# Moving one block's attention and its addition behind the first two tiles of the gated layer

## What is computed

```python
Q, K, V = x @ wq.T, x @ wk.T, x @ wv.T              # width 64
context = (Q @ (K.T V as D x D "energy")) * sqrt(3 / 64)
x = layernorm(x + context @ wo.T)
h = silu((x @ w1.T) * w1_s) * ((x @ w2.T) * w2_s)   # width 1024
h = gelu((h @ h1.T) * h1_s)                         # exact gelu
h = gelu((h @ h2.T) * h2_s)
x = layernorm(x + (h @ w3.T) * w3_s)
```

## Time and profile before

| | us |
|---|---|
| median of 3 runs | 651.08 |
| lowest and highest run | 650.98 to 651.11 |
| profiled run, whole | 650.84 |
| profiled run, span of the core | 649.0 |
| TensorE, products: busy | 637.2 (98%) |
| TensorE, weight loads: busy | 535.3 (82%) |
| VectorE busy | 492.3 (76%) |
| ScalarE busy | 408.6 (63%) |
| GpSimd busy | 282.5 (44%) |

### The profile page before, as it was taken

The page is one execution under the profiler, slowest core; times in us unless marked ns, Lnnn a source line. Parts: engine busy times, 40 slices in busy tenths (PEclk is TensorE's granted clock), DMA queues, the critical chain, the costliest instruction groups (busy, mean ns, idle before and its releaser), DMA issues.

```text
span 649.0 us, 9260 instructions
## 1 busy us (share of the span) xinstructions
PE 637.2 (98%) x3191; PEld 535.3 (82%) x3191; DVE 492.3 (76%) x721; ACT 408.6 (63%) x692; POOL 282.5 (44%) x226
## 2 busy tenths in 40 slices
PE   8989999999999999999999999999999999999995
PEld 6868788878879888888889888888879888888885
DVE  4677989989564997789655898698754899488476
ACT  5479689768671566558662657656763457566654
POOL 0367999493000762096000565078000367069025
PEclk9999999999999999999999999999999999999999
DMA  8998998973310046534330035634330015534201
GB/s 328 397 374 311 359 369 313 358 264 131 132 67 1 2 157 214 179 131 138 130 123 1 0 98 181 256 123 154 131 130 1 1 25 186 179 130 156 105 1 68
DMA packets 24371, 103.91 MB, mean 160 GB/s; under 512 B 2224, under 2 KB 3312, under 8 KB 16496
## 3 DMA queue, kind: packets, MB, share of 16 engines
q1 hardware_dynamic: 24032, 102.98, 44.7%
q10 hardware_dynamic: 288, 0.26, 0.1%
HBM read 87.51 MB, written 23.07 MB: 170 GB/s over the span
## 4 chain that ended last, share of the span: by engine, by line
PE 88%; DVE 5%; issue 2%; ACT 2%; DMA 1%; POOL 1%; SPq 0%; POOLq 0%; ACTq 0%; DVEq 0%
PE ps L1338 56%; PE ps L1281 17%; PE ps L1407 8%; DVE R L950 3%; PE ps L1181 2%; PE ps L1213 1%; PE ps L1164 1%; DMA xT<-in_xT 1%; PE ps L1430 1%; PE ps L1201 1%; ACT R L682 1%; PE ps L1189 1%; ACT junk L575 1%; POOL rstd L494 0%; DVE st L921 0%
## 5 line engine op out<-in xcount | busy, mean ns | idle before, releaser
L1338 PE MATMUL ps<-R,ring 128*128 128x512 f32 x1792 | 410.2, 390 | 0.2 <-DVE fsum L870 0.2
L1338 PEld LDWEIGHTS ps<-R,ring 128*128 128x128 f32 x1792 | 335.2, 188 | 69.9 <-DVE fsum L870 0.6
L950 DVE TENSOR_TENSOR R<-quarter,R 128x512 fp32r<-128x512 f32 x284 | 262.7, 948 | 57.3 <-ACT R L682 56.9
L682 ACT CAST R<-quarter 128x512 fp32r<-128x512 f32 x284 | 173.2, 617 | 30.3 <-POOL quarter L522 12.3
L1281 PE MATMUL ps<-x1T,w 128*128 128x512 f32 x512 | 119.1, 391 | 1.1 <-issue 0.4
L728 ACT ACTIVATE quarter<-U,sc 128x512 f32<-128x512 f32 x96 | 69.5, 724 | 73.0 <-DVE U L977 28.6
L1281 PEld LDWEIGHTS ps<-x1T,w 128*128 128x128 f32 x512 | 95.4, 188 | 22.6 <-ACT sg L646 1.2
L512 POOL TENSOR_TENSOR quarter<-quarter,quarter 128x512 f32<-128x512 f32 x32 | 50.5, 1578 | 94.8 <-ACT quarter L728 88.1
L463 POOL TENSOR_TENSOR ve<-mv,eps 128x4 f32<-128x4 f32 x14 | 5.6, 402 | 182.4 <-DVE mv L927 182.4
L646 ACT ACTIVATE sg<-ps,sc 128x512 f32<-128x512 f32 x64 | 44.2, 690 | 63.4 <-PE ps L1281 63.2
L698 ACT COPY U<-ps 128x512 f32<-128x512 f32 x96 | 56.3, 586 | 29.4 <-PE ps L1338 29.3
(11 more groups left out here) (85 smaller groups left out, 392.8 us busy)
## 6 DMA issues: line engine op xcount, KB each, us to landing
ring<-combos SPq DMA_DIRECT2D x56, 1024.0 KB, 5.0
combos<-unit SPq DMA_DIRECT2D x8, 1024.0 KB, 7.3
unit<-in_h1T SPq DMA_DIRECT2D x4, 1024.0 KB, 14.1
xr<-in_x_rows SPq DMA_DIRECT2D x8, 512.0 KB, 5.8
unit<-in_h2T SPq DMA_DIRECT2D x4, 1024.0 KB, 9.5
xT<-in_xT SPq DMA_DIRECT2D x7, 512.0 KB, 8.7
out<-xr SPq DMA_DIRECT2D x7, 512.0 KB, 3.3
w<-w_dram SPq DMA_DIRECT2D x3, 1024.0 KB, 7.8
```

Of the source, the lines that this page charges most:

```text
L682: nc.scalar.copy(R[slot_of(p, u)][:, 0, c, :], quarter[operand_home(p, u)][:, c, :]).then_inc(hi_done, 1)
L950: nc.vector.tensor_tensor(r[:, 1, c, :], quarter[operand_home(p, u)][:, c, :], r[:, 0, c, :].bitcast(f32), ALU.subtract).then_inc(lo_done, 1)
L1338: last = nc.tensor.matmul(ps[:, bank + j, :], w, view(R[slot_of(p, u)][:, part, k, :]), start=n in (0, 1, 5) and k == 0 and part == 0, sto ...
```

## The change

The two halves of block 1's attention leave the place in front of the gated layer. The transposes of tile 3 now follow those of tile 2 directly, half 0 stands behind tile 0 of the gated layer of block 0, and half 1 behind tile 1. On VectorE, the addition of block 1's attention moves behind the first gate, directly in front of the statistics. Nothing is added or removed, and the instructions themselves, their semaphores and their banks are the same. ScalarE, GpSimd and SP keep their order.

```diff
@@ VectorE
             normalised_tilewise(0, 0, attention_residual, lambda: flag_out(1))
             lo_of_transposed(0, 6)
-            residual1(1, 4)
             dve.wait_ge(cst_in, 16 * NCST)
             for j in range(HC):
                 gate(0, 0, j, A)
                 if j == 0:
+                    residual1(1, 4)
                     stats(0, 1, 1)
                 if j == 2:
                     normalise(0, 1, 1)
@@ TensorE
             def first_l1(view):
                 def side(t):
+                    if t == 0:
+                        attention_half(0)
+                    if t == 1:
+                        attention_half(1).then_inc(op_ready, 1)
                     if t == 2 * TR1_AFTER + 1:
                         pe.wait_ge(trlo_done, EC)
                         transposes(1, 6)
...
                 transposed_first(2)
-                attention_half(0)
                 transposed_first(3).then_inc(tr_ready, 1)
-                attention_half(1).then_inc(op_ready, 1)
                 l1(0, A, view, side)
                 l1(1, A, view, flag_side)
```

## The result

| | before | after |
|---|---|---|
| median, 22 runs each | 651.15 | 652.02 |
| lowest and highest run | 650.55 to 651.98 | 650.76 to 653.56 |
| profiled run, whole | 650.84 | 651.71 |
| span of the profiled run | 649.0 | 649.9 |

The ratio is 1.0014, with a 95% interval from 1.0008 to 1.0020: the change costs 0.9 us, between 0.5 and 1.3. The forecast was +0.60. Beside the median the spread has changed: 6 of the 22 runs of the changed kernel took 652.8 us or more, and none of the 22 before did. Two runs of kernels that come further down, at 1045.17 us (the filled kernel) and 780.9 us (the longer hole), were slow from end to end, at mean granted clocks of 0.57 and 0.77, and are left out of every median and count.

The account below looks back on a forecast made before the run. TensorE, busy 98% of the span, was taken as the bound, though it waits for other engines up to 42.46 us. Gain of 0.40 and cost of 1.00 gave +0.60, 651.7 us, range 650.9 to 652.4.

Parts of the forecast that it names:

- eight matmuls in the stream: Behind tiles 0 and 1 of the gated layer, the eight attention matmuls add 1.00 us to TensorE, 0.95 to 1.06.
- tile 3's transposes earlier: In front of the gated layer, without half 0 ahead, these transposes release ScalarE 0.40 us earlier, 0.35 at the low end.
- the addition behind the first gate: On VectorE, the second gate ends at 48.48; tile 7's slack falls from 0.88 to 0.16 us, nothing counted.
- given back at 139 us: Rival, chance 0.11: TensorE's 0.64 us wait at 139.04 takes most of the 0.60, giving 651.1 to 651.2.
- half 1's removal from the hole: Between 40.20 and 41.20 us, before the first product: gains nothing, since that product waits for ScalarE's cast anyway.
- the pinch: At tile 7, TensorE waits for VectorE's late second gate at the ring of four banks; up to 0.3 us in the range.
- no gain: Rival, chance 0.06: tile 3's transposes in front of the gated layer do not move; only +1.00 stands, 652.1.
- room: Rival, chance 0.08: the eight matmuls slip into the gated layer's stream free, leaving only -0.40, 650.7.
- the slower rival: Chance 0.11: over 1.3 us slower; the late second gate stops TensorE some 0.75 us at tile 7, 652.4 to 652.6.
- The third combination: On GpSimd, waiting for block 1's normalisation: moves from 49.75 to about 51.1, 1.3 us; the fourth starts at 56.54.
- The ring load that stood at 68.66: In SP's queue behind a combination's store: moves by up to 1.3 us, issued at 70, leaving 9 us to land.
- all later work keeps its spacing: After the stretch, the flag at 139 us moves by 0.60 too, its hole stays, and nothing is given back.

Follow-up runs that it names:

- the filled kernel: Changed kernel with both attention halves made a second time between tile 3's transposes and the gated layer: 651.48 us beside 651.08 before, ratio 1.0006.
- the longer hole: Changed kernel with three extra VectorE memsets in front of the low part of block 0's transposes: 654.73 us beside 651.08 before, ratio 1.0060.
- eight more: Changed kernel with both attention halves made a second time behind tile 10: 653.63 us, beside 651.08 before and 651.94 for the changed kernel.
- the order alone: Kernel before with only tile 3's transposes moved ahead of half 0, both halves still before the gated layer: 650.57 us beside 650.96, ratio 0.9994.
- the move of VectorE alone: Kernel before with only VectorE's addition moved behind the first gate, TensorE's order unchanged: 651.24 us beside 650.96, ratio 1.0006.
- the second series: The changed kernel itself timed once more, 11 runs: 651.94 us beside 651.08 for the kernel before, ratio 1.0014.
- the two kernels whose stream is earlier: Kernel before with only VectorE's addition moved, 651.24 us beside 650.96; changed kernel with half 0 in the hole before the gated layer, 651.08 beside 651.20.
- the kernel with half 1 inside tile 0: Kernel before with half 0 behind tile 3's transposes and half 1 inside tile 0: 650.44 us beside 650.96, again 650.78 beside 651.20.
- the three series of the two such kernels: Against the kernel before: tile 3's transposes ahead of both halves, 650.57 us; the same with half 1 inside tile 0, 650.44 and 650.78 us.

## Why the prediction was right, and what it lacked

| step | forecast | measured |
|---|---|---|
| eight matmuls in the stream | 1.00 | 0.99 in the changed kernel, 0.98 for eight more |
| tile 3's transposes earlier | -0.40 | -0.44 with the order alone; -0.48 from tile 2's transposes to the first product |
| the addition behind the first gate | hidden, 0.16 us of slack | no stop in the change; 0.44 and 0.47 where the stream is earlier |
| given back at 139 us | no | hole of 0.63 us, as before |
| TensorE's clock | not in the sum | fell in some executions; 1.2 us in the one that was profiled |
| time | +0.60 | +0.87 (0.5 to 1.3) |

**The price of the attention** was taken from two places where such matmuls stand in a running stream, and holds to 0.02 us. The figure of the Trainium skill that the prediction names beside them would have given 0.87; the rows decided rightly.

**The gain** was sized for the start of tile 2's transposes in that one profile, 39.33, 1.07 us behind the flag, which is the shortest such time of all twelve profiles: there, tile 3's readiness at 39.57 limits what can be gained. With the usual start at some 1.45 us behind the flag, both tiles are ready, and the whole of half 0 comes off: the first product stands 1.39 us behind tile 2's transposes instead of 1.87 (41.20 - 39.33), and the move of VectorE alone, with a start as late as the changed kernel's, has 1.87 too (40.98 - 39.11). So the steady part of the change is -0.48 + 0.99 = +0.51 us, which is the difference of the distances, 11.94 - 11.43, near the +0.40 of the filled kernel, whose ten runs show no upper tail. The steady part is still there at 139 us: in the first profile, from tile 2's transposes to the restart of the loads it is 139.80 - 39.56 = 100.24 us against 139.04 - 39.33 = 99.71, so +0.53.

**What failed** is the sentence that half 1's removal from the hole gains nothing and, by silence, costs nothing. It does cost: the empty hole is the end of a thin stretch, and 12 of 42 executions with it are in the upper tail, where the one profile shows a fall of the clock, at 1.2 us. That accounts for most of the rest between +0.5 and the median of +0.87: without the six runs of the tail the median is 651.72, +0.56, and in the second series, without three, 651.61, +0.53. It also makes the spread. The prediction had the granted clock of the kernel before, 0.999, in view, and did not ask what keeps it there. So the sum on TensorE is right, and that the median still lies in the range is partly luck: the room above +0.60 had been left for the pinch, which did not come.

**The chances** of the prediction do not add up as it says: forecast, given back, no gain and room are 0.64, 0.11, 0.06 and 0.08, together 0.89 and not 0.86.

**VectorE's part** was right in order and in numbers: the second gate at 47.92 (forecast 47.76), no stop at tile 7. That the slack is thin is shown by the two kernels whose stream is earlier. The mechanism of the slower rival, the pinch, is real, only not in this arrangement.

**GpSimd and SP.** The third combination starts at 50.89 instead of 49.75, the fourth at 56.69, on ScalarE's word as forecast (56.54):

```profile
50.89 1.29 POOL L452 TENSOR_TENSOR beside<-unit 128x512 f32<-128x512 f32 x1 [1.50 <-DVE xr L934]
...
56.69 1.32 POOL L452 TENSOR_TENSOR beside<-unit 128x512 f32<-128x512 f32 x1 [0.38 <-ACT junk L575]
```

The ring load that stood at 68.66 is issued at 68.71, not at 70 as I had feared: as far as this trace shows, it does not hang on that store. In the earlier trace rows and here ScalarE's activation is the link: 58.42 before, 59.17 after, 0.75 later, like TensorE's stream.

```profile
59.17 0.69 ACT L646 ACTIVATE sg<-ps,sc 128x512 f32<-128x512 f32 x1 [0.44 <-PE ps L1281]
```

**Given back.** In the first profile of the change, no. But in six of the later profiles TensorE also stops at 108 to 111 us, in front of the sixth product of the first hidden layer, for 0.17 to 1.05 us, on something that the trace does not name; roughly, the longer it stops there, the less it stops at 139 (0.62 down to nothing). The kernel with half 1 inside tile 0 has the longest of them,

```profile
108.43 3.50 PEld L1340 LDWEIGHTS ps<-R,ring 128*128 128x128 f32 x16 [1.05 <-issue]
```

and runs through at 139. These 1.05 us are 0.41 more than the hole of 0.64 in the kernel before, about what the front had gained in that execution. By the code a ring load is waited for there, and a sum made by another engine; which of them is late was not tried. The prediction's claim that all later work keeps its spacing was therefore too strong, though the sum held.

## What to carry to other kernels

In this kernel, work that stood in a hole of the bounding engine was free there; moved behind the hole it cost its full time in the stream, and moved behind what releases the next step it gave the rest: the transposes first, then both halves in the hole, is the arrangement that gives 0.4 us of distance without the cost. In time, the three series of the two such kernels are 0.4 to 0.5 us below before, and the interval of each takes in no change. Ask of a hole not only what fills it but what an empty one does: a thin stretch can cost TensorE its clock. And before a gain is sized from one profile, look whether the start it rests on is behind a branch or a flag read, which may stand elsewhere in the next execution.

## What the runs showed of the hardware

- The time from a flag written by VectorE to the first matmul of the branch that reads it differs from execution to execution: 1.07 to 2.04 us, mostly 1.4 to 1.55.
- TensorE's clock fell to its lower level for a few microseconds in the middle of a kernel that keeps it busy for 98% of the span: 0.57 of full speed granted from 42 to 46 us, at 1.2 us of time. The runs of the upper tail all have a mean clock of 0.996 or less for the whole run, but some ordinary runs have 0.996 as well.
- With the longer hole the fall (between 41.25 and 41.50 us) came before the longer wait, which began at 41.91, and the clock stayed at its lower level to 48 us.
- With matmuls that do nothing useful in the hole, none of ten runs is in the upper tail, and the median is 0.46 us below that of the same kernel without them.
